# Cross-attention with a two-expert layer on one core: where attended rows are divided by their sums, and when a tile's logits are taken

## The reference

```python
# B, Q, D = 32, 56, 512; context 1500 rows of 512; H, KV, HD = 16, 4, 96; 8 experts, 2 used
def _L0_xattn_ref(latents, context, Wq, Wk, Wv, Wo):
    hidden = jnp.concatenate([context, latents], axis=1)
    q = (latents @ Wq.T).reshape(b, q_len, H, HD)
    k = (hidden @ Wk.T).reshape(b, s_len, KV, HD)
    v = (hidden @ Wv.T).reshape(b, s_len, KV, HD)
    ...
    scores = jnp.einsum('bkgqd,bksd->bkgqs', q, k) * scale
    attn = jax.nn.softmax(scores.astype(jnp.float32), axis=-1).astype(q.dtype)
    out = jnp.einsum('bkgqs,bksd->bkgqd', attn, v)
    ...
    return out @ Wo.T
def _L0_ffn_ref(x, W_gate, b_gate, W_e, b_e):
    logits = x @ W_gate + b_gate
    _, top_idx = jax.lax.top_k(logits, TOP_K)
    y_all = jax.nn.relu(jnp.einsum('bsd,edh->bseh', x, W_e) + b_e)
    y = jnp.take_along_axis(y_all, top_idx[..., None], axis=2)
    return y.mean(axis=2)
x = x + _L0_xattn_ref(_layernorm(x, axis=-1), ctx_4096, ...)
x = x + _L0_ffn_ref(_layernorm(x, axis=-1), ...)
```

## Time and profile before

| | us |
|---|---|
| median of 3 runs | 3636.63 |
| lowest, highest | 3631.51, 3638.38 |
| the profiled execution, its own time | 3633.99 |
| span in its profile, first to last instruction | 3632.2 |
| TensorE busy in the span | 3529.3 (97%) |
| VectorE, ScalarE, GpSimd busy | 2147.2, 1707.4, 811.3 |

### The profile page before, as it was taken

One profiled execution on the slowest core, in us unless ns is written; L12 is line 12 of the kernel. 1 busy time (PEld: TensorE's weight loads), 2 busy tenths in 40 slices (PEclk: granted clock), 3 DMA queues, 4 the chain that ended last, 5 costly groups with the idle time before them and its releaser, 6 DMA issues. The chain is left out here.

```text
span 3632.2 us, 64988 instructions
## 1 busy us (share of the span) xinstructions
PE 3529.3 (97%) x22132; PEld 3242.5 (89%) x22132; DVE 2147.2 (59%) x3056; ACT 1707.4 (47%) x3204; POOL 811.3 (22%) x442
## 2 busy tenths in 40 slices
PE   8999999999999999999999999999999999688999
PEld 7889999999999999999999999999999999576887
DVE  5346666666666666666666666666666665455454
ACT  3235555555555555555555555555555555223222
POOL 0042222222222222222222222222222220430000
PEclk9999999999999999999999999999999999898999
DMA  6531111111111111111111111111111111673110
GB/s 220 190 127 50 49 49 49 49 49 49 49 49 49 49 49 49 49 49 49 49 49 49 49 49 49 49 50 49 50 49 49 49 49 31 176 196 128 35 35 32
DMA packets 304783, 240.27 MB, mean 66 GB/s; under 512 B 199394, under 2 KB 265186, under 8 KB 304114
## 3 DMA queue, kind: packets, MB, share of 16 engines
q1 hardware_dynamic: 304754, 239.92, 22.9%
HBM read 184.49 MB, written 55.34 MB: 66 GB/s over the span
## 5 line engine op out<-in xcount | busy, mean ns | idle before, releaser
L761 PE MATMUL ps_proj<-wv_hi,parts 128*125 128x384 f32 x3072 | 876.5, 339 | 0.0
L706 DVE TENSOR_TENSOR probs_lo<-probs,probs_hi 125x448 fp32r<-125x448 f32 (+1 forms) x896 | 686.7, 780 | 305.6 <-ACT probs_hi L633 297.6
L135 POOL TENSOR_SCALAR parts<-raw 128x1000 fp32r<-128x1000 f32 (+1 forms) x198 | 228.5, 1154 | 2336.8 <-PE ps_proj L761 2050.0
L748 PE MATMUL ps_proj<-parts,wk_hi 128*128 128x500 f32 x2304 | 712.3, 390 | 4.7 <-DVEq L661 4.7
L761 PEld LDWEIGHTS ps_proj<-wv_hi,parts 128*125 128x125 f32 x3072 | 560.3, 186 | 5.0
L625 ACT ACTIVATE probs<-ps_scores 125x448 f32<-125x448 f32 (+1 forms) x896 | 462.9, 517 | 123.0 <-DVE probs_lo L706 49.0
L761 PE MATMUL ps_proj<-wv_lo,parts 128*125 128x384 f32 x1536 | 519.1, 338 | 0.0
L137 POOL TENSOR_TENSOR parts<-raw,parts 128x1000 fp32r<-128x1000 f32 (+1 forms) x198 | 514.2, 2597 | 16.5
L748 PEld LDWEIGHTS ps_proj<-parts,wk_hi 128*128 128x128 f32 x2304 | 431.7, 188 | 94.4 <-DVEq L661 5.1
L617 ACT CAST values_hi<-ps_proj 125x384 fp32r<-125x384 f32 x384 | 184.4, 480 | 667.6 <-PE ps_proj L761 667.6
L633 ACT CAST probs_hi<-probs 125x448 fp32r<-125x448 f32 (+1 forms) x896 | 484.1, 540 | 28.3
(11 more groups left out here) (150 smaller groups left out, 5605.1 us busy)
## 6 DMA issues: line engine op xcount, KB each, us to landing
raw<-in_ctx SPq DMA_DIRECT2D x192, 500.0 KB, 3.6
qk_hi<-proj_out_hi SPq DMA_DIRECT2D x60, 224.0 KB, 2.0
qk_lo<-proj_out_lo SPq DMA_DIRECT2D x60, 224.0 KB, 2.2
queries_hi<-qk_hi SPq DMA_DIRECT2D x32, 336.0 KB, 3.5
queries_lo<-qk_lo SPq DMA_DIRECT2D x32, 336.0 KB, 3.5
att_t<-attended SPq DMA_DIRECT2D x128, 84.0 KB
raw<-att_t SPq DMA_DIRECT2D x7, 768.0 KB, 6.4
att<-att_t SPq DMA_DIRECT2D x7, 768.0 KB, 7.4
```

The lines of the kernel that those rows point to most:

```text
L706: dve.tensor_tensor(prs[1][0:R, u % PRING, 0:N], pr[0:R, u % PRING, 0:N], f(prs[0][0:R, u % PRING, 0:N]), ALU.subtract).then_inc(p_lo, 1)
L748: mm = pe.matmul(pproj[n % 2][:, 0:CS], w["wk"][a][:, j // 3, i * P:(i + 1) * P], ct[v][:, c, j // 3, :], start=(j == 0), stop=(j == 3 * K ...
L761: mm = pe.matmul(pproj[n % 2][0:VT, 0:KD], ct[a][:, t // VTC, j // 3, s], w["wv"][v][:, j // 3, :], start=(j == 0), stop=(j == 3 * KT - 1))
```

## The change

The division by the sums moves from the output stage to the attending stage. `store` writes the attended rows of a group undivided to a new DRAM tensor `att_raw` (a piece per partition and group instead of four), and the sums beside them. In the next batch SyncE runs `bring_back` after the first three context loads: it waits for the stores and for the last low part of the probabilities, loads the sums and all attended rows of the batch (96x896), the latter into two of the four buffers of `probs`; VectorE inverts the sums after its part of the fourth key tile; SyncE stores the inverses and loads them again, spread over 96 partitions, into the other two buffers; GpSimd multiplies (`normalize`), and `store_att` writes the result to the tensor that the output stage reads. ScalarE waits for this before the first and the third exponential of the batch. The last batch's return runs in the output stage, in buffers of its own. The spread inverses of the output stage, their loads and the multiply per tile go, and with them HEAD_PIECES and `scale`; ScalarE and VectorE split the loaded rows directly.

After the loop, three weight loads go out before the return of batch 30, and the stores of the last batch stand between the others. The first tile's rows are split by GpSimd at the end of the attending stage, into the place of the key weights (in the trace `wk_hi`, `wk_lo`), and TensorE's first output matmul waits for that alone. The last stores of the attending stage are waited for in the output stage. In `output(t)` the logits are those of tile t - 2, after matmul 10, and the transposes of t - 1 stand after matmul 31. The first tile of the next stage is split by GpSimd after output tile 12, also in the key weights' place.

```diff
+def load_back(sp, stream, scratch, b, home):
+    sp.dma_start(stream["sums"][:], scratch["z"][b].rearrange("(h q) -> h q", q=Q)).then_inc(stream["sums_loaded"], 16)
+    sp.dma_start(home[0], scratch["raw_att"][b]).then_inc(stream["back_loaded"], 16)
...
+def spread_inverse(sp, stream, scratch, b, home):
+    sp.wait_ge(stream["inverse_stored"], b * 16 + 16)
+    sp.dma_start(home[1], scratch["rz"][bass.ds(b, 1)].broadcast_to([HD, H * Q])).then_inc(stream["back_loaded"], 16)
+
+def normalize(pool, stream, b, home):
+    pool.wait_ge(stream["back_loaded"], b * 32 + 32)
+    pool.tensor_tensor(home[0], home[0], home[1], ALU.mult).then_inc(stream["normalized"], 1)
+
+def store_att(sp, stream, scratch, b, home):
+    sp.wait_ge(stream["normalized"], START + b + 1)
+    sp.dma_start(scratch["att"].rearrange("(h d) (b q) -> b d h q", d=HD, q=Q)[b],
+                 home[0].rearrange("d (h q) -> d h q", q=Q)).then_inc(stream["att_stored"], 16)
+
+def load_rows(sp, scratch, t, att, loaded):
+    sp.dma_start(att, scratch["att"].rearrange("(k p) r -> p k r", p=P)[:, :, bass.ds(t * P, P)]).then_inc(loaded, 16)
...
+        home = [pr[0:HD, n:n + 2, :].rearrange("p n c -> p (n c)") for n in (2, 0)]
...
                 def store(b, h):
                     sp.wait_ge(o_copied, START + b * KV + h + 1)
-                    sp.dma_start(att_d[b, :, h * G:(h + 1) * G, :],
-                                 osb[0:HD, h % 2, :].rearrange("d (h q) -> d h q", q=Q)).then_inc(stored[h % 2], 16)
...
+                    sp.dma_start(scratch["raw_att"][b, :, c], osb[0:HD, h % 2, :]).then_inc(stored[h % 2], 16)
+                    sp.dma_start(scratch["z"][bass.ds(b, 1), c], osb[HD:HD + 1, h % 2, :]).then_inc(stored[h % 2], 16)
+
+                def bring_back(b):
+                    for i in range(2):
+                        sp.wait_ge(stored[i], START + b * 64 + 64)
+                    sp.wait_ge(p_lo, START + b * NU + NU)
+                    load_back(sp, stream, scratch, b, home)
+                    store_inverse(sp, stream, scratch, b)
+                    spread_inverse(sp, stream, scratch, b, home)
+                    store_att(sp, stream, scratch, b, home)
...
-                for i in range(2):
-                    sp.wait_ge(stored[i], START + (B - 1) * 64)
-                load_sums(sp, stream, scratch, B - 2)
-                store_inverse(sp, stream, scratch, B - 2)
-                for n in range(LOADS):
+                for n in range(RAW):
                     load_wo(sp, stream, io, n)
-                for h in range(2):
-                    store(B - 1, h)
-
-                for i in range(2):
-                    sp.wait_ge(stored[i], START + (B - 1) * 64 + 32)
+                bring_back(B - 2)
+                load_wo(sp, stream, io, RAW)
+                store(B - 1, 0)
+                for n in range(RAW + 1, LOADS):
+                    load_wo(sp, stream, io, n)
+                store(B - 1, 1)
+
                 sp.wait_ge(stream["lo"], (B + 1) * LOADS)
-                sp.wait_ge(inverse_stored, (B - 1) * 16)
-                load_rows(sp, scratch, 0, *stream["first"], first_loaded)
+                sp.wait_ge(att_stored, START + (B - 1) * 16)
+                load_rows(sp, scratch, 0, stream["first"], first_loaded)
                 for h in range(2, KV):
                     store(B - 1, h)
-                for i in range(2):
-                    sp.wait_ge(stored[i], START + B * KV // 2 * 32)
...
-                pool.wait_ge(first_loaded, ROW_LOADS)
-                pool.tensor_tensor(stream["first"][0], stream["first"][0], stream["first"][1], ALU.mult).then_inc(first_scaled, 1)
+                (hi, lo), raw = stream["first_parts"], stream["first"]
+                pool.wait_ge(first_loaded, 16)
+                pool.tensor_scalar(hi, raw, 1.0, 0.0, ALU.mult, ALU.add).then_inc(stream["first_hi"], 1)
+                pool.wait_ge(stream["first_hi"], 1)
+                pool.tensor_tensor(lo, raw, f(hi), ALU.subtract).then_inc(stream["first_lo"], 1)
...
+                    if u == 0:
+                        act.wait_ge(normalized, START + b)
+                    if u == 2:
+                        act.wait_ge(att_stored, START + b * 16)
                     act.activation(pr[0:R, u % PRING, 0:N], psc[0:R, u % SBANKS, 0:N], ACT.Exp, scale=SCALE).then_inc(exp_done, 1)
...
+                            if (c, i) == (1, 0) and not first:
+                                invert_sums(dve, stream, b - 1)
...
-                        if u == 2 * UNITS and not first:
-                            invert_sums(dve, stream, b - 1)
...
-                def scale(i, s):
-                    pool.wait_ge(loaded[s], (i + s) * ROW_LOADS)
-
-                    pool.wait_ge(a_lo, START + 2 * i + s)
-                    pool.tensor_tensor(an[:], att[s], rz[s], ALU.mult).then_inc(scaled, 1)
+                normalize(pool, stream, B - 1, home)
...
+                def tile(t, s, more=True):
                     if more:
-                        if first:
-                            sp.wait_ge(a_lo, START + 1)
-                        else:
-                            sp.wait_ge(scaled, t + 1)
+                        if t > 0:
+                            sp.wait_ge(a_lo, START + t)
                         load(t + 2, s)
-
+                    if t > 1:
+                        store_x1(t - 2, s)
+                    if t > 0:
+                        store_xt(t - 1, 1 - s)
+                    if more:
                         sp.wait_ge(x1_done, t + 1)
                         load_x(t + 2, s)
...
                 def finish(t, s, more):
                     norm(t, s)
                     if more:
-                        split(t + 2, s, an[:])
-                    gate(t, s)
...
+                        split(t + 2, s)
+                    if not first:
+                        gate(t - 1, 1 - s)
...
-                        if not first and j == n // 2:
+                        if not (isinstance(t, int) and t < 2) and j == n // 4:
+                            logits(t - 2, s)
+                        if not (isinstance(t, int) and t < 1) and j == n - 6:
                             turn(t - 1)
-                        if not first and j == 3 * n // 4:
-                            logits(t - 1, 1 - s)
...
                 turn(OT - 1)
+                logits(OT - 2, 0)
                 logits(OT - 1, 1)
```

155 lines of the change are left out of this document (78 added, 77 removed).

## The result

The changed kernel takes 3578.73 us (median of 4 runs, 3575.25 to 3580.37), the kernel before 3634.07 us beside it (4 runs, 3626.30 to 3638.38). Of these 5 us, 2.6 are the distance at which the forecast put the median above the profiled execution (3633.99); with the fourth run the median of the kernel before came to 3634.07, and the distance was gone.

What follows compares the result with a forecast made beforehand. TensorE was taken to bound the attending batches, with holes before and waits in the output stage; 20.5 + 34.4 - 1.8 = 53.1 us gained from 3633.99, plus 2.6 for the median, gave 3584 us, range 3572 to 3604.

Steps and rivals of the forecast that it cites:

- tile 0: Start of the output stage: first output matmul at 3102.8 us instead of 3121.8.
- tiles 1 to 13: Output stage: 8.7 us for the first of them and twelve at 10.1, 129.9 instead of 164.3, 34.4 us gained.
- tile 0 itself: First output tile: 11.1 us long, kept from before because idle time ahead would leave a low clock again.
- the tail: Between last output tile and experts: an additional set of logits at low clock, 1.8 us lost; 0.8 at full clock.
- the way back: Attended rows' return through DRAM in the next batch, 31 times: taken as 0, within -0.1 and +0.3 us a batch.
- 18 us of cover: Each batch: return all in DRAM by 28 us, the first exponential that waits for it starts at 46.5.
- The third rival: Key tiles: GpSimd's multiply blocks VectorE, 43 us over 31 batches, 3627 us in all; chance 0.03.
- The output tiles: Output stage: spread inverses and multiply go, logits come one tile later; twelve tiles at 10.1 us, 121.2 together.
- The x1 ring: Output tiles: sum, norm, split, expert choice and x1 store take 9.1 to 10.6 us; upper end costs 6 us.
- the first rival: Output tiles miss 10.1 us, x1's cycle or late row loads set 11 to 12; 17 us, 3601; chance 0.16.
- what is late next before tile 0: End of attending: attending ends near 3095, GpSimd is late next, TensorE idles 8 us.
- the second rival: Last batch: GpSimd's six pairs delay the probabilities 3 to 6 us, late landing 2.7; 3590 us; chance 0.08.

Runs made afterwards that it cites:

- e5: Changed kernel with VectorE's inversion of the sums moved from after the fourth key tile to ahead of the fifth value tile; 3604.34 us, ratio 0.9920.
- e6: Changed kernel with VectorE's inversion of the sums moved to ahead of the eighth value tile; 3794.52 us in its one run.
- e2: Changed kernel with transposes, logits, choice of experts and stores of x1 in the output stage where they stood before; 3579.46 us, ratio 0.9852.
- e3: Kernel before with only the new order of transposes, logits and choice of experts; spread inverses and multiply stay; 3617.44 us, ratio 0.9955.
- e8: Changed kernel with GpSimd's subtractions of context, weights and first tile each cut in four; 3561.37 us, ratio 0.9806.
- e9: Changed kernel with GpSimd's subtractions cut in four, weight splits by context chunk, and all six weight loads ahead of the first store; 3552.07 us, ratio 0.9771.
- e11: Changed kernel with uncut GpSimd subtractions, weight splits by context chunk, and all six weight loads ahead of the first store; 3575.59 us, ratio 0.9834.

## Why the prediction was right, and where not

**The size.** 53.1 us were forecast and 55.1 measured on the spans. Term by term from the start of the last batch: tile 0 19.0 earlier forecast, 16.3 measured; tiles 1 to 13 in 129.9 us forecast, 128.4 measured; tile 0 itself 11.1 against 9.8; the tail (from the last tile to the experts) 1.8 lost against 0.6; the way back 0 against 0.04 us less per batch. The rest, 2.1 us gained ahead of the last batch and 1.3 lost in the experts' stage, no term stood for; it is as large as what executions differ by.

**The way back is free**, and step by step near the forecast. SyncE and GpSimd in the batch of the kernel after that starts at 1293.24:

```profile
1302.11 0.33 SPq L160 DMA_DIRECT2D sums<-row_sums  x1
...
1308.73 0.34 SPq L173 DMA_DIRECT2D inverse_sums<-inverse  x1
...
1315.52 0.35 SPq L191 DMA_DIRECT2D att_t<-probs  x1
```

```profile
1313.25 2.12 POOL L185 TENSOR_TENSOR probs<-probs 96x896 f32<-96x896 f32 x1 [40.32 <-DMA probs<-inverse_sums]
```

The loads left 8.9 us into the batch (9 forecast), the store of the inverses at 15.5 (14.3), the multiply ran from 20.0 to 22.1 (2.12 us long, 2.0 forecast), and the exponential that waits for it came at 46.6. The 18 us of cover were counted to the end of the last store. e5 and e6 show the price beyond it: 0.75 us a batch, then 6.9. The third rival, which would have cost 43 us, did not come: beside the multiply VectorE works on PSUM, its instructions there took 0.68 and 1.20 us as ever, and the batch did not grow.

**The output tiles** took 9.98 us each from tile 2 on (119.8 for twelve; 121 forecast), and tile 1 8.6 (8.7). The wait for ScalarE's copied rows is gone from TensorE's list. The x1 ring that was to set the lower end is there, but only VectorE feels it: its sum waited for the store of x1 five times, 11.1 us in all and 2.3 at the longest, and TensorE never for it. So the first rival did not come either. The sum was right in size here, but the text put both edits into one term; e2 and e3 show that removing the multiply and the spread inverses carries most of it and the later logits 3.8 us, once the chain is short.

**The step that failed is what is late next before tile 0.** The prediction put the end of attending near 3095 and made GpSimd's split of the first tile the last thing, 8 us after it in one piece. GpSimd kept that timetable: its six splits ended at 3090.2 (3091.6 forecast), the rows landed for 3094.9 (3096.9), both halves were done at 3100.2 (3102.3). But attending ended only at 3101.07, six us later than forecast and 0.9 behind GpSimd. TensorE idled not once but seven times, 7.0 us in all, each time for VectorE's low part of the probabilities (the first of them, 0.46 us, is in every batch, with 0.38), and then 2.04 us for the border, for which half a microsecond stood in the sum. I had the row that said so, five subtractions in 5.59 us next to GpSimd, and used it only to price the multiply in the key tiles. GpSimd's split of the rows itself falls on the last units of the batch, and that it would hold up VectorE there stood in no term. It is the second rival's mechanism, but at the end of the batch it cost little: counted from the last batch's start tile 0 came 2.7 us later than forecast, where that rival gave 6. GpSimd's chain itself ended 97.7 us after the batch's start, just as forecast. In e8, where it was the last thing, tile 0 followed it 0.8 us later; here tile 0 waited for the end of attending and the border behind that, 3.2 us. So the late end of attending cost only some 2.4 us; for the rest it took the place of idle time. That both chains ended within a microsecond of each other was luck: no term had the one through VectorE.

**Two sizes, both of the clock.** It was low only from 3099.9 to 3106.7, so for the first 3.3 us of tile 0, where it had been low for the first 6.1 before. Tile 0 took 9.8 us instead of the 11.1 carried over from before, 1.3 us better than forecast. And the tail cost 0.6 instead of 1.8, since the logits of tile 12, at 3245.23 below, still ran at full clock: 0.96 us for eight passes. Those of tile 13, at 3246.85, already ran at the low one.

```profile
3244.74 0.66 PE L1153 MATMUL ps_t<-ident_g,xn_g 128*128 128x128 f32 x4 [2.95 <-DVE xn_g L1108]
3245.23 0.96 PE L1161 MATMUL ps_g<-w_gate,xt_g 128*128 128x8 f32 x8
3246.12 0.38 PE L1162 MATMUL ps_g<-b_gate,ones_g 1*128 1x8 f32 x2
3246.85 1.42 PE L1161 MATMUL ps_g<-w_gate,xt_g 128*128 128x8 f32 x6 [0.35 <-DVE logits L1113]
```

**Slips.** The slices with a low clock are 35 and 37, not 35 and 36. For a way back that is late enough to make the kernel slower, each of the four transfers would have to take 8.6 us, not over 9 (46.5 + 2 - 28 us more, in four parts). Neither changes the forecast.

**Left open.** From the end of tile 13 to the end of the program the kernels differ by up to 4.4 us (332.6 in e2, 333.6 before, 333.8 in e9, 335.5 after, 337.0 in e3). Where the low clock falls behind the last tile differs between them too; no run here holds that place fixed, so what part it has is not shown.

## What to carry to other kernels

A hole ahead of a stage can have two chains behind it that end almost together, here GpSimd's loads and splits on one side and VectorE's subtractions on the other: price them separately. e8 and e11 shortened one each, and tile 0 started 103.6 and 96.2 us after the last batch's start; only e9, which shortened both, brought it to 92.8, right behind a batch of the usual length. Before two edits with the same aim are added up, ask what each is worth once the other is made; the late logits gave 21 us in the output tiles alone and 4 after the chain had become short. Work that is put on GpSimd beside VectorE should be held against the operands of VectorE's instructions at that moment, and cut short where they have two in SBUF.

## What the runs showed of the hardware

**A long instruction of GpSimd costs VectorE more than the same work in short ones.** With GpSimd's subtractions cut in four, VectorE's longest subtraction fell from 2.56 to 1.39 us and TensorE's waits for it from 18.7 to 0.3 us, although GpSimd itself was busy 28.5 us a batch (e9) instead of 24.6. This shortened every batch by 0.64 us, 20 us in all, in a loop in which TensorE was busy 89.3 of 90.0 us; expected were 0.36, the hole before VectorE's low part. By the windows of the kernel after and of e9 half of it was TensorE's idle time (0.69 to 0.31 us a batch), the other half its recorded busy time (89.31 to 88.99), for which no row names a reason. The Trainium skill (SBUF — State Buffer, the part on engine-side contention) says that the loser of the shared port pair blocks for the whole instruction of the other; the longest times agree with that: 2.56 us beside whole subtractions of 2.6 us, and 1.39 us, which is its own 0.6 and most of one of the cut pieces (3.1 to 4.2 us for four). The longest of the last batch took 3.6 us beside GpSimd's subtraction of 3.67. The maxima of VectorE, which read PSUM, were not lengthened to more than 0.7 us beside GpSimd.

**Tile 0 paid the same for a low clock behind many short holes and behind one long one.** In the kernel after 7.0 us of holes in seven pieces and 2.0 at the border stood ahead of it; in e8 one hole of 13.5 us. In both the clock was low for the first 3 us of tile 0, its mean 0.83 and 0.84, and the tile took 9.8 us. Before, with holes of 10.81, 1.26 and 12.77 us ahead, the clock was low for the first 6.1 us of the tile and its mean 0.76. In the output tiles e3 ran at 1.00 with 11.8 us of idle time in 143.4, where the kernel before had 0.92 with 19.7 in 164.3; whether the amount or the length of the single holes decides that, no run here separates.
